# Attention kernel on one core: P V in five blocks and row sums in two blocks per batch, with a ring of five probability slots

## The reference, cut to what matters

```python
h = rms_norm(layernorm(x), norm_weight)
q, k, v = split(h @ w_qkv.T)            # 16 heads x 64
q, k = rope(q), rope(k)
k, v = concat(pm, k), concat(pm, v)     # 260 keys
attn = softmax(causal(q @ k.T * 64**-0.5))
x = x + (attn @ v) @ w_out.T
# ffn on layernorm(x): for each of the 32 steps
c = sigmoid(xt@wf.T + c@uf.T + bf) * c + sigmoid(xt@wi.T + c@ui.T + bi) * tanh(xt@wc.T + c@uc.T + bc)
x = x + tanh(xt @ wo.T + c_final @ uo.T + bo)
```

## Time and profile before

| | |
|---|---|
| median of 3 runs | 1124.64 us (1124.19 to 1130.9) |
| profiled execution | 1127.17 us |
| its span, first to last instruction | 1125.4 us |
| mean granted clock of PE | 0.988 |
| busy: PE, DVE, ACT, POOL | 1079.8, 934.1, 698.1, 633.8 us |
| costliest group: L1173 PE, P V | 224.7 us, 2048 matmuls |
| L1194 PE, row sums | 82.6 us, 2048 matmuls |

### The profile page before, as it was taken

How to read it: one execution, slowest core, us unless ns; L and a number is a source line. 1 busy time by engine, 2 the same in 40 slices (tenths; PEclk the granted TensorE clock), 3 DMA queues, 4 the chain that set the end, 5 groups by cost and what they waited for, 6 DMA issues and landing times.

```text
span 1125.4 us, 47265 instructions
## 1 busy us (share of the span) xinstructions
PE 1079.8 (96%) x18443; PEld 814.4 (72%) x18443; DVE 934.1 (83%) x3306; ACT 698.1 (62%) x1575; POOL 633.8 (56%) x819
## 2 busy tenths in 40 slices
PE   4979999999999999999999999999999999999996
PEld 2557777777777777777777777777777777777775
DVE  6778888888888888888888888888887889888645
ACT  3746665666666666666666666566675666666634
POOL 4546565556656555665565576565566566656510
PEclk8989999999999999999999999999999999999998
DMA  6222433432333333233333333333332333333215
GB/s 208 105 85 88 115 112 110 120 115 86 95 112 115 116 115 116 78 103 111 116 116 115 108 96 92 111 112 111 115 98 87 113 109 110 111 111 103 71 23 150
DMA packets 78031, 120.52 MB, mean 107 GB/s; under 512 B 13041, under 2 KB 35954, under 8 KB 77682
## 3 DMA queue, kind: packets, MB, share of 16 engines
...
...
## 4 chain that ended last, share of the span: by engine, by line
PE 66%; DVE 14%; DMA 10%; SPq 3%; issue 3%; POOL 1%; ACT 1%; DVEq 0%; POOLq 0%; ACTq 0%
PE bank_pv L1173 12%; PE bank L1065 12%; PE bank_st L1129 9%; DMA rope_c<-rope_b 7%; PE bank_sum L1210 6%; PE bank_sum L1194 5%; PE bank_sm L1104 4%; DVE masked L835 4%; PE bank L1087 4%; DMA linv_scratch<-linv 3%; PE bank L1084 2%; PE bank L1312 2%; PE bank L1314 2%; PE bank_st L1133 2%; SPq L312 2%
## 5 line engine op out<-in xcount | busy, mean ns | idle before, releaser
L419 POOL TENSOR_TENSOR qk<-rope_a,rope_c 128x512 f32<-128x512 f32 x256 | 341.0, 1332 | 301.2 <-DMA rope_c<-rope_b 293.4
L835 DVE CUSTOM_DVE_ANT_0 masked<-bank_sm,mask_q 128x132 bf16<-128x132 f32 (+1 forms) x1024 | 307.1, 354 | 16.5 <-PE bank_sm L1104 15.7
L412 POOL TENSOR_TENSOR prob<-prob 128x264 f32<-128x264 f32 x256 | 209.5, 818 | 120.0 <-ACT prob L559 113.4
L824 DVE TENSOR_TENSOR rope_a<-bank,cos 128x512 f32<-128x512 f32 x256 | 174.0, 680 | 121.5 <-PE bank L1065 80.7
L544 ACT ACTIVATE qk_h<-qk 128x512 f16<-128x512 f32 x256 | 160.4, 626 | 167.9 <-POOL qk L419 167.2
L559 ACT ACTIVATE prob<-bank_st 128x784 f32<-128x784 f32 x256 | 209.0, 817 | 60.3 <-PE bank_st L1138 59.6
L1173 PE MATMUL bank_pv<-prob,v_sb 128*64 128x256 f32 (+1 forms) x2048 | 224.7, 340 | 0.8 <-DVE raw L851 0.6
L1129 PE MATMUL bank_st<-qk 64*64 64x256 f32 (+3 forms) x4096 | 186.2, 299 | 0.2
L1129 PEld LDWEIGHTS bank_st<-qk 64*64 64x64 f32 x4096 | 167.7, 134 | 9.2 <-issue 0.9
L825 DVE TENSOR_TENSOR rope_b<-bank,sin 128x512 f32<-128x512 f32 x256 | 173.7, 679 | 0.0
L1173 PEld LDWEIGHTS bank_pv<-prob,v_sb 128*64 128x64 f32 x2048 | 124.3, 136 | 54.6 <-issue 1.3
...
## 6 DMA issues: line engine op xcount, KB each, us to landing
rope_c<-rope_b SPq DMA_DIRECT2D x512, 128.0 KB, 2.4
rinv<-linv_scratch SPq DMA_DIRECT2D x124, 256.0 KB, 4.7
...
v_end<-v_end_scratch SPq DMA_DIRECT2D x64, 8.0 KB
v_sb<-pm_v SPq DMA_DIRECT2D x63, 8.0 KB
```

The source lines that it names most:

```text
L412: G.tensor_tensor(prob_2[:, s % 4, :, :], prob[:, s % 4, :, 0:NT - Q1], prob[:, s % 4, :, C0 + Q1:SCOL], ALU.add).then_inc(S["prob_added"], 1)
L419: G.tensor_tensor(qk[:, s, :].rearrange("p (u n) -> p u n", u=2)[:, :, 0:NT], rope_a[:, (NPAIR * j + s) % 3, :].rearrange("p (u n) -> p u ...
L824: V.tensor_tensor(rope_a[:, (NPAIR * j + s) % 3, :], proj_bank(j, s)[:, :], cos[:, :], ALU.mult)
L835: ins = V.tensor_tensor_reduce(masked[:, e, c0:c0 + n], ps_sm[:, e, c0:c0 + n], mask_q[:, c0:c0 + n], 1.0, LOWEST, ALU.add, ALU.max, top[: ...
```

## The change

`attend` now works in five blocks per batch, `sums` in two. `PV_AT` names the pairs of each block by slot: pair 7 of the batch before in slot 0, then pairs 0 and 1 in slot 2, 2 and 3 in slot 4, 4 in slot 5, 5 and 6 in slot 7. A second pair of a block goes to columns 256 to 511 of `ps_pv`, and `raw_copy` copies a block with one instruction. The sums of pairs 0 to 3 both stand in slot 4, those of pairs 4 to 7 both in slot 0 of the next iteration. Since a pair's probabilities are held longer, the ring has five slots, given by `SLOT`, and `sums_before` works out which sums must be done before a slot is written again. To make room, `x_end`, the normalised `x_end`, `pmk_raw` and `cf_hl` now share memory with `raw`, `th` and `ga`.

```diff
+SLOT = (3, 0, 1, 2, 4, 0, 1, 2)
+PV_AT = {0: (7,), 2: (0, 1), 4: (2, 3), 5: (4,), 7: (5, 6)}
...
-        prob = sb("prob", [P, 4, 2, SCOL], f32)
-        prob_2 = sb("prob_2", [P, 4, 2, NT - Q1], f32)
+        prob = sb("prob", [P, 5, 2, SCOL], f32)
+        prob_2 = sb("prob_2", [P, 5, 2, NT - Q1], f32)
...
-        cf_hl = sb("cf_hl", [P, 2, NT], f16)
+        cf_hl = ga[:, :].bitcast(f16).rearrange("p (u n) -> p u n", u=2)
...
+        def sums_before(bj, s):
+
+            last = max([s0 for s0 in range(s) if SLOT[s0] == SLOT[s]], default=None)
+            if last is not None:
+                return 4 * bj + last // 2 + 1
+            last = max(s0 for s0 in range(NPAIR) if SLOT[s0] == SLOT[s])
+            return 4 * (bj - 1) + last // 2 + 1
...
-                wait(pool, S["sum_ready"], 4 * bj + (s - 4) // 2 + 1)
+                wait(pool, S["sum_ready"], sums_before(bj, s))
...
-                wait(act, S["sum_ready"], 4 * bj + (s - 4) // 2 + 1)
+                wait(act, S["sum_ready"], sums_before(bj, s))
...
-            def raw_copy(bj, par, s):
-                act.wait_ge(S["pv_ready"], NPAIR * bj + s + 1)
+            def raw_copy(bj, par, pairs_of):
+                s, n = pairs_of[0], len(pairs_of)
+                act.wait_ge(S["pv_ready"], NPAIR * bj + s + n)
...
-                A.activation(raw[:, par, s, :], ps_pv[:, 0:NT], ACT.Copy, scale=1.0 / RS).then_inc(S["raw_done"], 1)
+                A.activation(raw[:, par, s:s + n, :].rearrange("p s q -> p (s q)"), ps_pv[:, 0:n * NT], ACT.Copy,
+                             scale=1.0 / RS).then_inc(S["raw_done"], n)
...
-                        raw_copy(j - 2, p, NPAIR - 1)
+                        raw_copy(j - 2, p, PV_AT[0])
...
-                    if s >= 1 and b:
-                        raw_copy(j - 1, 1 - p, s - 1)
+                    if s in (2, 4, 5, 7) and b:
+                        raw_copy(j - 1, 1 - p, PV_AT[s])
...
-            def attend(bj, s):
+            def attend(bj, s, at):
                 pe.wait_ge(S["exp_done"], NPAIR * bj + s + 1)
 
-                wait(pe, S["raw_done"], NPAIR * bj + s)
+                if at == 0:
+                    wait(pe, S["raw_done"], NPAIR * bj + s)
...
                     if s == 0 and c:
-                        attend(j - 2, NPAIR - 1)
-                    if s >= 1 and b:
-                        attend(j - 1, s - 1)
+                        attend(j - 2, NPAIR - 1, 0)
+                    if s in (2, 4, 5, 7) and b:
+                        for i, pair in enumerate(PV_AT[s]):
+                            attend(j - 1, pair, i * NT)
                     if s == 0 and c:
+                        sums(j - 2, 2)
                         sums(j - 2, 3)
...
-                    if s in (2, 4, 7) and b:
-                        sums(j - 1, (2, 4, 7).index(s))
+                    if s == 4 and b:
+                        sums(j - 1, 0)
+                        sums(j - 1, 1)
```

More of the change, by code:

```diff
@@ L114, in build @@
         e1_e2 = sb("e1_e2", [P, QT + 1], f32)
-        xn0 = sb("xn0", [P, (QT + 1) * D], f32)
+        xn0 = sb("xn0", [P, QT * D], f32)
         rope_a = sb("rope_a", [P, 3, 2 * NT], f32)
@@ L139, in build @@
         raw = sb("raw", [P, 2, NPAIR, NT], f32)
+        x_end = raw[:, 0, 0, 0:D]
         linv = sb("linv", [P, NT], f32)
@@ L147, in build @@
         th = sb("th", [P, GATES, NT], f32)
+        xn_end = th[:, 0, 0:D]
+        pmk_raw = th[:, 1, 0:NPAIR * NPM]
         ga = sb("ga", [P, NT], f32)
@@ L278, in _ @@
             const_f32(sin[:, :], "sin").then_inc(S["ld_rope"], 16)
-            sp.dma_start(x_end[:, :], x_last).then_inc(S["ld_end"], 16)
+            sp.dma_start(x_end, x_last).then_inc(S["ld_end"], 16)
             sp.dma_start(c_raw, consts_cast).then_inc(S["ld_c"], 16)
-            sp.dma_start(pmk_raw[:, :], pm_k).then_inc(S["ld_small"], 16)
+            sp.dma_start(pmk_raw, pm_k).then_inc(S["ld_small"], 16)
             sp.dma_start(bo_sb[:, :], bo_row).then_inc(S["ld_small"], 16)
@@ L511, in _ @@
             act.wait_ge(S["ld_small"], 64)
-            pk = pmk_raw[:, :].rearrange("p (c n) -> p c n", c=NPAIR)
+            pk = pmk_raw.rearrange("p (c n) -> p c n", c=NPAIR)
             cast(A.copy(qk[:, :, NT:NT + NPM], pk))
@@ L750, in moments, with normalise @@
                 return last
-            def normalise(q, src):
-                return V.tensor_scalar(xn0[:, q * D:(q + 1) * D], src, sh_mv[:, q, 0:1], sh_r[:, q:q + 1],
+            def normalise(q, src, to):
+                return V.tensor_scalar(to, src, sh_mv[:, q, 0:1], sh_r[:, q:q + 1],
                                        ALU.subtract, ALU.mult)
@@ L779, in _ @@
             for q in range(QT):
-                last = normalise(q, x_sb[:, 0, q * D:(q + 1) * D])
+                last = normalise(q, x_sb[:, 0, q * D:(q + 1) * D], xn0[:, q * D:(q + 1) * D])
             last.then_inc(S["h_xn"], 1)
@@ L788, in end_stats @@
                 dve.wait_ge(S["ld_end"], 16)
-                link(V.bn_stats(sh[:, QT, :], x_end[:, :]))
+                link(V.bn_stats(sh[:, QT, :], x_end))
                 V.bn_aggr(sh_mv[:, QT, :], sh[:, QT, :]).then_inc(S["end_stats"], 1)
@@ L793, in end_norm @@
                 dve.wait_ge(S["end_rstd"], 1)
-                normalise(QT, x_end[:, :]).then_inc(S["end_xn"], 1)
+                normalise(QT, x_end, xn_end).then_inc(S["end_xn"], 1)
             def end_low():
@@ L1172, in attend @@
                         col = (2 * s + e) * DH
-                        last = T.matmul(ps_pv[OWN[e], q0:NT], v_sb[:, kc, col:col + DH], prob[:, s % 4, e, c0:c0 + NT - q0],
+                        last = T.matmul(ps_pv[OWN[e], at + q0:at + NT], v_sb[:, kc, col:col + DH], prob[:, SLOT[s], e, c0:c0 + NT - q0],
                                         start=(kc == 0), stop=(kc == 1))
@@ L1191, in sums @@
                     for r in range(4):
-                        slot = (2 * g + r // 2) % 4
+                        slot = SLOT[2 * g + r // 2]
                         src = prob_2[:, slot, r % 2, :] if part else prob[:, slot, r % 2, C0:C0 + Q1]
@@ L1372, in body @@
                         pe.wait_ge(S["end_xn"], 1)
-                        T.transpose(ps_sum[:, 0:P], xn0[:, QT * D:(QT + 1) * D], ident_f[:, :]).then_inc(S["end_tr"], 1)
+                        T.transpose(ps_sum[:, 0:P], xn_end, ident_f[:, :]).then_inc(S["end_tr"], 1)
                     if j == 0 and s in (6, 7):
```

6 lines of the change are left out of this document (2 added, 4 removed).

## The result

The changed kernel takes 1143.52 us (median of 4 runs, 1142.48 to 1146.75); the kernel before, run beside it, 1127.66 (4 runs, 1124.19 to 1130.9). The ratio is 1.0146 with an interval of 1.01 to 1.0192: slower by 15.9 us. The median of the kernel before is 3.0 us higher here than the 1124.64 that the forecast started from, because a fourth run was added; so the distance of the forecast time, 6.4 us, looks better than that of the step. The profiled execution of the changed kernel took 1146.75 us; its span, 1144.9, is 19.5 above that of before.

What follows compares the result with a forecast made beforehand. The prediction took PE's work and its waits for DVE's maxima at two walls as the bound. Stretch D 18.9 plus Stretch B 6.4 gave +25.3 us on the median 1124.64, so 1150 us, range 1140 to 1160.

Steps and rivals of the forecast that it cites:

- The walls: L1104 to L1112, slots 1 to 3 and 6 to 7: DVE's maxima keep them at 5.76 and 1.83 us; PE waits.
- wall C: L1104 of slot 6 to L1112 of slot 7: stays 1.83 us; PE, without its P V block, waits 0.81.
- Stretch D: L1112 of slot 7 to L1104 of next slot 1, PE's work: +0.59 us a loop, 32 times, 18.9 us.
- Stretch B: L1112 of slot 3 to L1104 of slot 6: +0.36 us clean, 0.22 on average as late loops absorb it; 6.4 us.
- The ends: Start and drain outside the 28 steady loops: Stretch D was counted 32 times, Stretch B 29 times.
- ScalarE, forecast 0: Wider raw copies delay qk_h, but L1104 reads that two slots later, over 6 us away: cost 0 on the path.
- 1 (faster): Rival: no waits at the walls, only fewer changes of shape count, -17 us, 1108 us; chance 4%.
- 2 (a wall gives way): Rival: for instance DVE reaches wall C 0.8 us earlier, a loop gains 0.14, +4 us, 1129 us; chance 6%.
- 4 (the clock): Rival: PE's clock is cut because PE idles, 1.6 us a loop, some 50 in all, 1200 us; chance 3%.
- 5 (a new wait on ScalarE): Rival: late raw copies or the ring delay P V or exp, up to 0.7 us in some loops, 1158 to 1170; 8%.
- 3 (B adds nothing, 1144 us): Rival: more loops are set by the rope-swap DMA than counted, Stretch B adds 0 everywhere, +19 us; chance 12%.
- The main case: Both walls stand and Stretch B is paid in loops not late: 1150 us, own range 1145 to 1156; chance 67%.

Runs made afterwards that it cites:

- the second execution: The changed kernel run once more, unedited, as the base for other edits: 1143.54 us, 1.0142 of the kernel before.
- the light kernel: The changed kernel with DVE's row maxima cut to reductions of 8 columns, result not the reference's: 1120.18 us, 0.9912 of the kernel before.
- the last table above: The changed kernel with P V (0, 1), (2, 3), (4, 5), 6, 7 in slots 2, 4, 6, 7, 0, sums in slots 2, 4, 6, 0: 1127.85 us, 0.9976.

## Why the prediction was right, and where its sizes were off

**The walls: right.** L1104 to L1112 stayed at 5.76 and 1.82; the weight load's waits came to 65.6 us in 62 waits (60 to 80 forecast), the matmul's to 53.4 (about 50), PE's idle time grew by 41.9 (42), the granted clock of the steady loop is 1.00. That the walls cause the loss isn't only argued: filling wall C with one block took back 12 us, and the clean loop, 32.54, is the 32.51 of the walls' step to 0.03.

**Stretch D, forecast +0.59, measured +0.51.** The terms of the sum that were mis-sized are the prices of grouping. The double P V block takes 538.50 - 537.04 = 1.46 us (1.464 to 1.467 over the run), so the second pair cost 0.65, not 0.71; a double block of sums takes 524.77 - 523.75 = 1.02, so the second cost 0.44, not 0.46. I had read the price of a change of shape (0.10 to 0.12) from blocks followed by another operation of the same shape but of other width and operands. Two equal blocks save 0.15 and 0.14 a time. PE's busy time fell by 22.4 us rather than 17 for the same reason. In 28 loops this is 2.2 us of the miss.

**Stretch B, forecast +0.36 clean and +0.22 on average, measured +0.29 and +0.02.** The clean part is the same two prices again (-0.81 + 0.65 + 0.44 = +0.28). The average is where most of the miss lies, 28 x 0.20 = 5.6 us: late loops absorb what PE's path gains in length. The step named this and counted it too small. It took the loops of one execution and let 0.22 through. In the two executions compared only 0.02 came through: the kernel before had three loops in which the late rotation started after 12 us, at B + C of 19.3 to 19.6, and the changed one none (latest 11.03). Whether that is chance isn't settled. For chance: the rule of the third wall on all 196 loops gives 17.48 for a path of 17.31 and 17.30 for 17.03, a step of +0.18. Against it: D (14.3), the drain (1.1) and the lead-in of the second execution (1.7) make 17.1 us without it; with 28 x 0.18 = 5.0 more it would be 22.1, while the medians are 15.9 apart, with an interval of 11.3 to 21.7. The pieces come from single executions, so this speaks for a smaller share and doesn't exclude a part of the 0.18. In the executions compared B adds about nothing, and of the step it is the share let through that was too large.

**The ends, forecast +2.6 beyond the 28 loops, measured +4.7.** 1.1 us in the drain; 3.6 in the lead-in, of which about 2 go with the longer stretch at half clock (above), and 1.7 is what the second execution shows.

The 5.8 us between 25.3 and the profiled 19.5 are then 2.2 + 5.6 - 2.1, but for rounding. Another 3.7 lie between the profiled executions and the medians: that of the changed kernel was 3.2 above its median, that of before 0.5 below.

**ScalarE, forecast 0: right in this kernel (1.2 us in 2 waits of L1117, where it was 1.2 in 3), by a cover the prediction didn't see.** It looked for the reader behind qk_h, two slots away. The near one is the copy of the transposed maxima, 0.45 us late once DVE no longer holds the transposition. It was seen only where the transposition isn't held: in the light kernel, and at slot 7 with blocks 4 and 5 in slot 6 (0.23 in the loop shown).

**The rivals.** 1 (faster) and 2 (a wall gives way) fell with the unchanged 5.76 and 1.82, and 4 (the clock) with the 1.00, although PE idles 1.50 us a loop. 5 (a new wait on ScalarE) did not show in the changed kernel. 3 (B adds nothing, 1144 us) had a chance of 12% and is what stretch B did; that its time is the measured 1143.5 nearly to the digit is in part luck, since the smaller D and the longer ends cancel and the median it started from was 3.0 lower. The main case was right on what the walls do and wrong on this absorption.

**Open.** Why the swap of the rope halves lands, and with it the rotation of slot 5 starts, anywhere between 8.6 and 12.3 us after the transposition; splitting the broadcast ahead of it brought the landing forward by 2.2 us on average but left DVE's own work in its place. Whether the kernel before really has more of the very late ones than the grouped kernels, for which one profiled execution of it is too little; two kernels built on the changed one have one each, at 12.00 (the last table above) and 12.96 (the light one). Whether a table that keeps slot 6's work ahead of the late rotation would win was not tried.
